# One-head attention weights split in rows and transposed by DMA, and unread TensorE products at the borders of six blocks

## The reference

```python
query = image @ Wq + bq                 # 2048 x 256, after a layer norm
key, value = text @ Wk + bk, text @ Wv + bv
scores = einsum('bqh,bkh->bqk', query, key) / sqrt(256)
weights = softmax(scores, axis=-1)      # 2048 x 1601
x = x + einsum('bqk,bkh->bqh', weights, value)
```

## Time and profile before

| | us |
|---|---|
| runs of the kernel | 1739.45, 1741.71, 1742.35 |
| median | 1741.71 |
| profiled execution, its own time | 1739.82 |
| span of its records | 1737.9 |
| PE busy in the span | 1646.7 (95%) |
| DVE busy | 1540.1 (89%) |
| ACT busy | 1313.0 (76%) |
| POOL busy | 332.1 (19%) |

### The profile page before, as it was taken

One profiled execution on the slowest core, in us unless ns is written; L12 is line 12 of the kernel. 1 busy time (PEld: TensorE's weight loads), 2 busy tenths in 40 slices (PEclk: granted clock), 3 DMA queues, 4 the chain that ended last, 5 costly groups with the idle time before them and its releaser, 6 DMA issues. The chain is left out here.

```text
span 1737.9 us, 36736 instructions
## 1 busy us (share of the span) xinstructions
PE 1646.7 (95%) x14560; PEld 656.0 (38%) x14560; DVE 1540.1 (89%) x2285; ACT 1313.0 (76%) x2590; POOL 332.1 (19%) x594
## 2 busy tenths in 40 slices
PE   6899999999999999999999999999989997889995
PEld 3533222332233223223322222222235554667773
DVE  6867999999999999999999999999958886888876
ACT  4514989889988998898899999999975564545554
POOL 5800012112211302201201001010014443400000
PEclk9956999999999999999999999999999999999997
DMA  4001002001110210100321011010020000000001
GB/s 142 13 1 13 13 13 32 14 14 32 32 13 13 32 19 13 26 14 14 78 58 20 19 20 20 14 26 14 14 78 10 1 1 1 1 1 2 2 1 49
DMA packets 93755, 38.71 MB, mean 22 GB/s; under 512 B 83152, under 2 KB 91856, under 8 KB 93328
## 3 DMA queue, kind: packets, MB, share of 16 engines
q1 hardware_dynamic: 92880, 34.98, 9.5%
q10 hardware_dynamic: 704, 1.38, 0.2%
HBM read 14.07 MB, written 2.10 MB: 9 GB/s over the span
## 5 line engine op out<-in xcount | busy, mean ns | idle before, releaser
L938 DVE TENSOR_REDUCE mxp<-ps_m 128x2 f32<-128x1024 f32 (+2 forms) x928 | 1052.3, 1200 | 56.8 <-PE ps_m L728 52.7
L874 ACT ACTIVATE work<-ps_s 128x512 f32<-128x512 f32 x1856 | 1005.4, 596 | 106.6 <-PE ps_s L752 79.9
L778 PE MATMUL ps_av<-work,vst 128*32 128x256 f32 x7424 | 593.9, 392 | 14.7 <-ACT avs L881 12.3
L752 PE MATMUL ps_s<-qb,k_stack 50*128 50x512 f16 x1856 | 570.7, 383 | 0.0
L728 PE MATMUL ps_m<-k_stack,qa 48*128 48x512 f16 (+1 forms) x2048 | 539.0, 368 | 2.3 <-PEq L1083 1.6
L778 PEld LDWEIGHTS ps_av<-work,vst 128*32 128x32 f32 x7424 | 147.1, 108 | 386.8 <-ACT work L874 332.2
L752 PEld LDWEIGHTS ps_s<-qb,k_stack 50*128 50x128 f16 x1856 | 119.1, 94 | 378.5 <-ACT work L874 333.8
L728 PEld LDWEIGHTS ps_m<-k_stack,qa 48*128 48x128 f16 x2048 | 107.1, 94 | 39.7 <-issue 21.9
L606 POOL TENSOR_SCALAR mtmp<-negm 128x16 f32<-128x16 f32 x32 | 8.2, 256 | 584.2 <-DVE negm L943 584.1
L592 POOL COPY vst<-v_rows 128x1024 f32<-128x1024 f32 (+1 forms) x32 | 30.6, 957 | 136.9 <-PE ps_av L778 136.8
L803 PE MATMUL ps_s<-spare,work 112*128 112x256 f32 x96 | 55.7, 701 | 0.0
(11 more groups left out here) (425 smaller groups left out, 1966.7 us busy)
## 6 DMA issues: line engine op xcount, KB each, us to landing
x_res<-in_x SPq DMA_DIRECT2D x4, 512.0 KB, 8.0
w_experts<-in_w_experts SPq DMA_DIRECT2D x1, 2048.0 KB, 8.1
out<-x_res SPq DMA_DIRECT2D x8, 256.0 KB, 2.2
v_rows<-in_ctx_c SPq DMA_DIRECT2D x1, 1664.0 KB, 8.6
work<-in_ctx_t SPq DMA_DIRECT2D x1, 1456.0 KB, 15.7
ctx_n<-in_ctx_n SPq DMA_DIRECT2D x1, 1248.0 KB, 7.2
w_qkv<-in_w_qkv ACTq DMA_DIRECT2D x1, 768.0 KB, 8.3
w_qkv<-in_w_qkv SPq DMA_DIRECT2D x1, 768.0 KB, 4.1
```

The source lines that it names most:

```text
L752: pe.matmul(ps_s[:, bank, :], STACKS[part(n)][rows, group(n) * PAIRS + j, t * P:t * P + P], qb[n % 2][rows, :, j, :], start=True, stop=Tru ...
L778: m = pe.matmul(ps_av[32 * h:32 * h + 32, cols], vst[n % 2][:, t, h, :], pbuf[(tau[n] + t) % 2][:, h, cols], start=(t == 0 and half == 0), ...
L874: a.activation(pbuf[g % 2][:, h, :], ps_s[:, b, :], ACT.Exp, scale=factor).then_inc(s["exp"], 1)
L938: v.tensor_reduce(dst, src, AX.X, ALU.max).then_inc(s["mred"], 1)
```

## The change

In `cross_one_head` PE's transposes of the weights go. ACT casts `pn` where it lies, in rows (`high`, two pieces of 1024 and 577 columns), DVE subtracts in rows (`low`, two pieces, both inputs in SBUF), and SP transposes each half of the result with one DMA of 128 x 1664 f16 into `pht` or `plt` (two buffers each; `ph` and `pl` have one). The values of a tile are multiplied one step later, the output two steps later. The normalisation of the input and its product with the side row move from DVE to POOL. At the borders of blocks PE gets products into banks that nobody reads (`idle_products`): 15 at the end of `self_qkv` (3, then 3, 1, 1 and 7 by step), 5 at the end of `attentions`, 8 before the last `outer` of `projection_experts_queries`, 10 after the first queries of `cross_one_head` and 6 at its end, 10 at the head of `quantised_ffn`; 54 in all, each of 512 columns.

```diff
+def idle_products(pe, out, lhs, rhs, count):
+    for _ in range(count):
+        pe.matmul(out, lhs, rhs, start=True, stop=True)
@@ attentions, tensor
             results(NCH - 1)
+            idle_products(pe, ps_s[:, 0, :], identh[:, :], qa[0][:, 0:2, :, :].rearrange("p a j b -> p (a j b)"), 5)
@@ self_qkv, tensor
+FILL = (3, 1, 1, 7)
+            def unused(count):
+                idle_products(pe, prod[0][:, 0, :], identh[:, :], ks[:, 0, 0:512], count)
...
                 if 0 <= n - T < TAIL_KV:
                     context(n - T)
+                if n == T - 1:
+                    pe.wait_ge(s["qmul"], T - 1)
+                    pe.wait_ge(s["vout"], T - 1)
+                    pe.wait_ge(s["kout"], 4)
+                    unused(3)
+                if n >= T:
+                    unused(FILL[n - T])
                 if 0 <= n - LAG - 1 < T:
@@ projection_experts_queries, tensor
+                if n == T + LAG:
+                    pe.wait_ge(s["gused"], T)
+                    idle_products(pe, logit[:, :], weh[:, 0, 0:P], weh[:, 0, 0:512], 8)
                 if n - LAG - 1 >= 0:
                     outer(n - LAG - 1)
@@ cross_one_head, gpsimd
+            for n in range(T):
+                if n >= 2:
+                    g.wait_ge(s["xtr"], n - 1)
+                if n == FIRST_T:
+                    g.wait_ge(s["rstd"], 1)
+                if n > 0:
+                    g.tensor_scalar(xn[n % 2][:, :], x[:, n, :], mean[:, n:n + 1], rstd[:, n:n + 1], ALU.subtract, ALU.mult)\
+                     .then_inc(s["xn"], 1)
+                g.wait_ge(s["xn"], n + 1)
+                g.wait_ge(s["r"], 2 * n)
+                g.tensor_tensor(prods[:, :], xn[n % 2][:, :], side[:, 0:D], ALU.mult).then_inc(s["r"], 1)
@@ cross_one_head, sync
+            for n in range(T):
+                e.wait_ge(s["ph"], 2 * n + 2)
+                if n > 0:
+                    e.wait_ge(s["hi"], 16 * n)
+                if n >= 2:
+                    e.wait_ge(s["av"], n - 1)
+                e.dma_start_transpose(pht[n % 2][:, :, :], ph[:, :]).then_inc(s["hi"], 16)
+                e.wait_ge(s["pl"], 2 * n + 2)
+                if n > 0:
+                    e.wait_ge(s["lo"], 16 * n)
+                e.dma_start_transpose(plt[n % 2][:, :, :], pl[:, :]).then_inc(s["lo"], 16)
@@ cross_one_head, tensor
+            unused(10)
             for n in range(T):
-                turn_p(n, 0)
-                turn_p(n, 1)
...
+                if n + 1 < T:
+                    score(n + 1, 0)
                 if n + 2 < T:
                     turn_x(n + 2)
+                if n >= 2:
+                    turn_o(n - 2)
+                if n + 1 < T:
+                    score(n + 1, 1)
+                if n >= 2:
+                    project(n - 2)
+                if n + 1 < T:
+                    score(n + 1, 2)
+                    score(n + 1, 3)
                 if n + 2 < T:
                     query(n + 2)
+                if n >= 1:
+                    values(n - 1, range(TM))
+            values(T - 1, range(0, 6))
+            turn_o(T - 2)
+            values(T - 1, range(6, TM))
+            project(T - 2)
             turn_o(T - 1)
             project(T - 1)
+            unused(6)
@@ cross_one_head, scalar
+            def high(n, k):
+                a.wait_ge(s["ex"], 2 * n + k + 1)
+                if n > 0:
+                    a.wait_ge(s["hi"], 16 * n)
+                a.copy(ph[:, PIECES[k]], pn[n % 2][:, PIECES[k]]).then_inc(s["ph"], 1)
@@ cross_one_head, vector
+            def low(n, k):
+                v.wait_ge(s["ph"], 2 * n + k + 1)
+                if n > 0:
+                    v.wait_ge(s["lo"], 16 * n)
+                v.tensor_tensor(pl[:, PIECES[k]], pn[n % 2][:, PIECES[k]], ph[:, PIECES[k]], ALU.subtract).then_inc(s["pl"], 1)
@@ quantised_ffn, tensor
             s["sum"].open(pe)
+            idle_products(pe, ps_i[:, :], identb[:, :], wq[:, :, :].rearrange("p k n -> p (k n)"), 10)
             pe.wait_ge(s["am"], 2)
```

145 lines of the change are left out of this document (51 added, 94 removed).

## The result

| | before | changed |
|---|---|---|
| median of the runs | 1741.12 us (1739.45 to 1742.35, 4 runs) | 1723.37 us (1721.32 to 1725.35, 4 runs) |
| ratio to before | | 0.9898, 95% interval 0.9883 to 0.9914 |
| profiled execution: time, span | 1739.8, 1737.9 | 1723.2, 1721.1 |

The change gains 17.7 us where I had forecast 44; the sign was right, and 1723 lies in the range (1687 to 1727) only because rival A was taken into it. Where the executions of one kernel fall into two groups, some 28 us apart, they are given one by one, because the difference between the groups is what is studied.

The account below looks back on a forecast made before the run. PE was taken as the bound, at half clock in the opening of `attentions` and in the one-head block. Terms -29 - 1.5 - 0.5 - 12 - 0.4 = -43.4 from 1739.8 gave 1696.4, forecast as 1697 us; range 1687 to 1727.

Parts of the forecast that it names:

- rival A: Clock falls at the first block's border or in the thin stream behind it, stays down; about 1726 us; chance 0.13.
- (a): Fifteen unread products ending `self_qkv` hold PE's clock, so DVE bounds the opening of `attentions`; -29 us (0 to -32.7).
- (b): Five unread products at the end of `attentions` hold the clock for the dense work behind; -1.5 us (0 to -1.7).
- (e): Ten unread products at the head of the last block, beside DVE's chain; -0.4 us (-0.5 to +1.8).
- (c): Eight unread products before the projection block's last `outer` cover 1.7 us before the barrier; -0.5 us (0 to -2).
- (d): One-head block with DMA transposes: tiles of 9.1 us instead of 10.46, longer end; net -12 us (-13.4 to +3).
- tail: One-head block from tile 15's scores to the border: 19.5 us before, forecast 29.0 with the deeper pipeline.
- Rival B: One-head block: DVE's `low` and POOL collide on SBUF, up to 1.1 us a tile; 1712 us; chance 0.09.
- Rival C: One-head block: a tile's two DMA transposes served one behind the other, 6.6 us each; 1759 us, slower; chance 0.05.

## Why the prediction was wrong

Right in sign, and wrong by the largest term, (a). Of the others, (b) and (e) came within 0.5 us, (c) gave nothing, and (d) gave 3.4 us more than forecast.

- **(a), the opening: the step that failed.** Forecast -29, measured 0. The sentence that failed is "What the products leave is nearer to the first, so I take the hold". For the border itself it came true: PE idles 0.45 us there and the clock stays at full. I compared that remaining pause with other pauses and stopped there. The next pause, 0.99 us long and two units on, was not in my sum; I only took off 1.5 us for "PE's start ahead of DVE" without asking what PE does when it has run ahead and DVE is late: it stands still. The trace of before could not show it as a wait, as PE was at half clock and late itself, but it showed DVE's three steps at 80.11 to 82.0 us, and two banks of 0.95 us each at full clock are used up by 82.2. The term's size was right: with the pause gone, the opening takes 45.7 us, the first scores start at 126.0 (forecast near 127), and the time is 1692 (forecast 1697).
- **Rival A** (0.13) named the place, "in the thin stream behind it", and the time, 1726. Its reason was wrong: the thin stream holds the clock by itself. The clock fell for the pause.
- **(b)** -1.5, measured -1.0. The clock held there. **(c)** -0.5, measured 0: it fell at 1473 all the same. Up to the linear attention 1.5 us more came from a fall at 1459 which did not happen this time, and 1.4 were given back in the linear attention, where one happened at 1514 (6.8 us at half). Neither stretch was touched by the change; these falls move from kernel to kernel, and I had no term for them.
- **(d), the one-head block.** Forecast -12, measured -15.4. From the scores of tile 1 to those of tile 15: 123.6 us (1536.53 to 1660.11), forecast 124.8, before 145.7 (1537.27 to 1682.92). The prediction had 146.4 for it, 14 times 10.46, and so 0.8 us too little for the old tail; in the net the two errors cancel. The period is 8.90 and all PE's; my 9.0 for the loop over ACT and DVE was too long, since PE never waits for it (DVE is busy for 7.9 us of the period, ACT for 5.1). The tail took 26.6 us against a forecast of 29.0. 1.5 of the 2.4 were for a clock that falls in 5 us of idle time before the last values; the idle time measured 1.31, because the values of the tile before stand in it (they start at 1672.7 and end at 1676.1), and the clock did not fall there. I had let them run earlier. 0.4 us was lost ahead of tile 1's scores. The fall at 1545, 3.4 us at half, was in no term.
- **Rival B**, the ports: the collision happened in 11 of POOL's 15 steps, and struck POOL, whose step took 2.26 us in most of them (2.80 to 2.87 in three) instead of 1.22 beside DVE's two-input `low`; DVE's own pieces kept their length (1.24 and 0.77). The rule of the Trainium skill that I had weighed describes that they exclude each other. Its order, that the second to issue waits, the rows do not bear out: POOL's record starts at 1599.43, 0.07 us ahead of DVE's, and POOL waited (its spans are rough). POOL had the time. It cost the block nothing. The collision that did damage was one that I had not looked for, DVE's scaling beside POOL's memset at 80.6 us.
- **Rival C**: 4.0 and 4.3 us to land (medians), never waited for in the loop. They are served one behind the other, as the rival said, but in 2.1 us each and not 6.6.
- **(e)** -0.4, measured -0.3. The ten products end at 1689.2, as DVE's chain asks PE for `fall` at 1689.3. The clock fell later all the same, at 1695.

## What to carry to other kernels

When a change is to hold the clock over a border, follow the engine past the border at the new speed, with the buffers that it has, until it is in step with its partner: the first stall behind the border belongs to the same sum, and it is hidden in the old trace as long as the engine is slow. Look first for work on the partner that nobody needs yet; moving it, or the memset that holds it up, can be worth more than the products that fill the gap. And measure such a kernel more than four times: one that leaves the clock near the edge has two times, here 28 us apart, and the first four runs of the changed kernel, all within some 4 us, did not show it.

## What the runs showed of the hardware

- One program on one chip can hold the clock in one execution and lose it in the next: 1693.1 and 1723.4 us for the same kernel, with 1.6 us of idle at one border.
- Two stalls of 0.45 and 0.99 us, separated by 2.0 us of full work, brought the clock from 2.4 to 1.2 GHz in 9 of 10 executions; 0.45 and 0.55 did in none of 5.
- The clock stayed at the low level for 78 us of an opening in which the profile shows PE without a gap; the same opening with two products of 512 columns more in each unit had it back at full 6.9 us after the fall (80.7 to 87.6).
- A DVE scaling of 128x256 f32 in SBUF took 1.00 us beside a GpSimd memset that had begun 0.04 us before, 0.28 without it. GpSimd's scaling of the same size took 2.26 beside DVE's two-input subtraction of 1024 columns, 1.22 alone.
- A DMA transpose of 128x1664 f16 was issued in 1.5 to 1.9 us and landed 4.0 to 4.3 us behind its issue (medians; up to 6.0). Two moved their data in 4.1 us and three in 6.3, one behind the other, 2.1 us each.
